# A fused decoder layer on one Trainium2 core: all convolution taps as matmuls, the first B and C and the last expert weights by matmuls, constants over two queues, own places for the end chunks

## What is computed

```
xz = x @ W_in;  x_b, z = split(xz)                      # 256 channels each
xc = silu(conv_b + sum_k xpad[:, k:k+T] * conv_w[:, k])  # 4 taps, causal
proj = xc @ W_xproj                                      # 8 + 16 (B) + 16 (C)
delta = softplus(proj[:8] @ W_dt + b_dt)
h = exp(delta * A) * h + (delta * xc) * B                # per channel and state
y = sum_s h * C + D_param * xc
x = layernorm(x + (y * silu(z)) @ W_out)
...
hidden = silu(x @ gate) * (x @ up)                       # 16 experts of 64
out = sum_e combine[e] * (hidden[e] @ down[e]) + shared expert
```

## Time and profile before

| what | us |
|---|---|
| median of 3 runs (lowest to highest) | 1175.11 (1173.61 to 1177.04) |
| the profiled execution | 1174.27 |
| its span in the trace | 1172.2 |
| PE busy | 1055.3 (90%) |
| DVE busy | 1065.3 (91%) |
| ACT busy | 993.9 (85%) |
| POOL busy | 972.0 (83%) |
| mean granted clock of PE, share of full | 0.967 |

### The profile page before, as it was taken

The page is one execution under the profiler, slowest core; times in us unless marked ns, Lnnn a source line. Parts: engine busy times, 40 slices in busy tenths (PEclk is TensorE's granted clock), DMA queues, the critical chain, the costliest instruction groups (busy, mean ns, idle before and its releaser), DMA issues. The chain is left out here.

```text
span 1172.2 us, 18321 instructions
## 1 busy us (share of the span) xinstructions
PE 1055.3 (90%) x5831; PEld 742.9 (63%) x5831; DVE 1065.3 (91%) x1492; ACT 993.9 (85%) x2176; POOL 972.0 (83%) x590
## 2 busy tenths in 40 slices
PE   4677888989899998989989899998989999898998
PEld 2465665666666666666666666666666667666665
DVE  2999999999999999999999999999999999999622
ACT  6788898989989898998979898898989889898443
POOL 0687888979988897988979798898989889897944
PEclk9677999999999999999989999999999999999999
DMA  6443444545564444555534455654545655443322
GB/s 173 175 171 146 163 164 158 164 164 189 198 196 156 172 162 153 188 207 190 182 127 168 163 189 187 204 175 162 159 160 178 208 187 182 144 166 144 122 68 74
DMA packets 84112, 194.50 MB, mean 166 GB/s; under 512 B 17288, under 2 KB 47936, under 8 KB 67632
## 3 DMA queue, kind: packets, MB, share of 16 engines
q1 hardware_dynamic: 84016, 193.33, 48.8%
HBM read 179.14 MB, written 5.77 MB: 158 GB/s over the span
## 5 line engine op out<-in xcount | busy, mean ns | idle before, releaser
L936 POOL TENSOR_TENSOR read<-state,bc_all 128x1024 f32<-128x1024 f32 x256 | 604.0, 2364 | 140.8 <-DVE state L805 126.3
L805 DVE TENSOR_TENSOR_SCAN state<-decay,drive_bank 128x512 f32<-128x512 f32 (+1 forms) x464 | 594.7, 1313 | 0.4
L755 ACT ACTIVATE decay<-delta,a_neg 128x252 f32<-128x252 f32 x1024 | 424.6, 494 | 0.9
L797 DVE TENSOR_TENSOR drive_bank<-dx_bank,bc_all 128x512 f32<-128x512 f32 (+1 forms) x496 | 328.9, 701 | 27.6 <-DMA bc_all<-bc_dram 25.8
L372 PE MATMUL y_bank<-ident,read 128*128 128x128 f32 x2048 | 282.6, 283 | 44.9 <-POOL read L936 44.8
L372 PEld LDWEIGHTS y_bank<-ident,read 128*128 128x128 f32 x2048 | 241.7, 146 | 118.9 <-POOL read L936 80.8
L977 POOL TENSOR_TENSOR hid<-gu,comb_all 128x512 f32<-128x512 f32 (+1 forms) x136 | 165.0, 1214 | 22.5 <-DVE gu L897 18.8
L363 PEld LDWEIGHTS down_bank<-down_w,hid 128*128 128x128 f32 x1024 | 132.3, 196 | 37.0 <-issue 28.1
L363 PE MATMUL bank<-x2T,gate_w 128*128 128x512 f32 (+1 forms) x272 | 135.0, 588 | 9.8 <-ACT delta L735 4.3
L363 PE MATMUL down_bank<-down_w,hid 128*128 128x128 f32 x1024 | 139.1, 281 | 3.0 <-POOL hid L977 1.4
L363 PE MATMUL bank<-x2T,up_w 128*128 128x512 f32 (+1 forms) x272 | 130.0, 571 | 0.8 <-ACT xc L711 0.7
(11 more groups left out here) (128 smaller groups left out, 1385.0 us busy)
## 6 DMA issues: line engine op xcount, KB each, us to landing
bc_all<-bc_dram SPq DMA_DIRECT2D x128, 1024.0 KB, 5.3
comb_all<-comb_dram SPq DMA_DIRECT2D x240, 128.0 KB, 3.0
x_in<-in_x_dram SPq DMA_DIRECT2D x15, 256.0 KB, 5.7
ctx_in<-in_ctx_dram SPq DMA_DIRECT2D x15, 256.0 KB, 6.4
k_pair<-k_pair SPq DMA_DIRECT2D x30, 128.0 KB, 2.1
q_pair<-q_pair SPq DMA_DIRECT2D x30, 128.0 KB, 2.5
out_dram<-y_out SPq DMA_DIRECT2D x15, 256.0 KB, 3.1
comb_all<-comb_dram SPq DMA_DIRECT2D x32, 64.0 KB, 2.6
```

What stands on the lines that cost most here:

```text
L755: done = e.activation(seqs(decay_t[j % DECAYS][:, i, h, :])[:, :, 1:T], seqs(delta[c % 2][:, h, sub * SUB:(sub + 1) * SUB])[:, :, 1:T], AC ...
L797: e.tensor_tensor(drive_bank[:, a:b, :, :], dx_bank[:, :, :].unsqueeze(1).to_broadcast(shape), bc_all[group % BC_BUFS][:, 0, PAIR * i + a: ...
L805: e.tensor_tensor_scan(states(state_t[j % STATE_BUFS], a, b), states(decay_t[j % DECAYS], a, b), states(drive_bank, a, b), 0.0, ALU.mult, ...
L936: e.tensor_tensor(read_t[j % READS][:, :, :, :], state_t[j % STATE_BUFS][:, :, :, :], bc_all[group % BC_BUFS][:, 1, PAIR * i:PAIR * (i + 1 ...
```

## The change

- **Taps.** w_tap holds both halves; tap_mm is due twice a chunk, four matmuls each. xb_mm, conv_bias, tap1 to tap3 and the conv tile are gone; both xc are one silu with the bias.
- **First B and C.** For the first sub, PE broadcasts the first eight rows (four of B, four of C) of proj to all partitions by matmuls with a column of the identity, into down_bank and y_bank, and DVE copies them to bc_all. proj and the first dx of chunk 0 are made on DVE, dx straight into dx_bank. The first B and C load is gone.
- **Last weights.** In the last chunk the routing weights are spread by matmuls with a selector, built on DVE from the identity, into drive_bank, dx_bank and y_bank; DVE makes the eight hid products there. Its comb store and loads are gone.
- **Constants.** ident, a_log and conv_b are issued by ACT; the rest stays on SP, part of it moved to ticks -15, -7 and 1. The loads have semaphores of their own. Three tiny activations (warm) load function tables early. The centrings move to ticks 7 and 15.
- **Places.** AT has five columns: normal, last, last but one, first, second. EXP_AT too. Four drives of 16 are whole (one before) and four scans (three before).

The diff, cut to its core:

```diff
@@ -42,85 +44,101 @@
-    "tap_mm": [(-38, -40)],
-    "xb_mm": [(-43, -41)],
...
+    "tap_mm": [(-43, -42, -41, -60, -40), (-38, -38, -37, -41, -35)],
+    "xc": [(-36, -35, -39, -29, -44), (-34, -32, -32, -25, -43)],
...
-WHOLE_DRIVES = (7,)
-WHOLE_SCANS = (3, 6, 14)
+WHOLE_DRIVES = (6, 7, 9, 13)
+WHOLE_SCANS = (5, 8, 9, 14)
...
+        selector = decay_t[0][:, :, :, :].rearrange("p i h n -> p (i h n)")
+
+        tap_rows = read_t[0][:, :, :, :].rearrange("p i h n -> p (i h n)")[:, 0:INNER * TAPS]
...
+        def last_weight(pair):
+
+            if pair < PAIR * HALVES:
+                return drive_bank[:, pair // HALVES, pair % HALVES, :]
+            return dx_bank[:, pair % HALVES, :] if pair < PAIR * HALVES + 2 else y_bank[:, pair % HALVES, :]
...
-                for c in due(tick, "tap_mm"):
-                    bank = take(("xb", c, 0), tick, 3)
+                for c, h in due(tick, "tap_mm"):
+                    bank = take(("xb", c, h), tick, 3)
                     w.wait_ge(S["xT"], at(c))
-                    w.wait_ge(S["w_tap"], 1)
+                    w.wait_ge(S["w_tap"], h + 1)
                     for n in range(TAPS):
-                        done = mm(seqs(bank.t[:, 0:width(c)])[:, :, n:T], w_tap[:, TAPS - 1 - n, :],
+                        done = mm(seqs(bank.t[:, 0:width(c)])[:, :, n:T], w_tap[:, h, TAPS - 1 - n, :],
                                   seqs(xT[c % 3][:, 0:width(c)])[:, :, 0:T - n], start=n == 0, stop=n == TAPS - 1)
...
-                for c in due(tick, "xb_mm"):
-                    bank = take(("xb", c, 1), tick, 6)
...
+                    if c == 0:
+                        for two in (0, 1):
+                            for pair in (0, 1):
+                                w.wait_ge(S["bc_copy"], 2 * two + pair - 1)
+                                for i in range(PAIR):
+                                    row = DT_RANK + GROUP * pair + PAIR * two + i
+                                    done = mm((down_bank, y_flat)[pair][:, i * SUB:(i + 1) * SUB],
+                                              ident[0:PROJ, row:row + 1].to_broadcast([PROJ, P]), proj[0:PROJ, 0:SUB])
+                                done.then_inc(S["bc_mm"], 1)
...
+                for c, pair in due(tick, "weight_mm"):
+                    if c < LAST:
+                        continue
+                    w.wait_ge(S["combT"], at(c))
+                    w.wait_ge(S["state"], PAIR * STEPS)
+                    w.wait_ge(S["y_gated"], ALL_SUBS)
+                    w.wait_ge(S["selector"], 1)
+                    mm(last_weight(pair), selector[0:EXPERTS, pair * P:(pair + 1) * P],
+                       combT[:, 0:SUB]).then_inc(S["weight_mm"], 1)
...
+            e.dma_start(ident[:, :], io["c_ident"]).then_inc(S["ident"], 16)
+            e.dma_start(a_log[:, :, :], io["L0_attn_A_log"].rearrange("(h p) n -> p h n", p=P)).then_inc(S["a_log"], 16)
+            per_channel(e, conv_b, io["L0_attn_conv_b"], S["conv_consts"])
...
-            def tap(c, n):
-
-                w.wait_ge(S["conv_bias"], at(c))
...
-                stt(out, seqs(bank_of["xb", c, 1][:, 0:width(c)])[:, :, 0:T - n], conv_w[:, 1, TAPS - 1 - n:TAPS - n], out,
-                    ALU.mult, ALU.add).then_inc(S["conv_tap"], 1)
...
+                    bc_copy(0, 0)
+                    w.wait_ge(S["delta"], 2)
+                    w.wait_ge(S["xc"], HALVES)
+                    e.tensor_tensor(dx_bank[:, :, :], xc[0][:, :, 0:SUB], delta[0][:, :, 0:SUB],
+                                    ALU.mult).then_inc(S["first_dx"], 1)
+                    bc_copy(0, 1)
+                    bc_copy(1, 0)
+                    bc_copy(1, 1)
...
-                        (0, -3, ((w_out[:, :, :], 0, HALVES), (down_w[:, :, :], HALVES, PAIRS))),
-                        (1, 5, ((w_qkv[:, 2:3, :], HALVES + PAIRS, 1), (shared_w[:, 2:3, :], HALVES + PAIRS + 1, 1)))):
+                        (0, 7, ((w_out[:, :, :], 0, HALVES), (down_w[:, :, :], HALVES, PAIRS))),
+                        (1, 15, ((w_qkv[:, 2:3, :], HALVES + PAIRS, 1), (shared_w[:, 2:3, :], HALVES + PAIRS + 1, 1)))):
...
+                    index = pair + 1
+                    w.wait_ge(S["gu"], at(c, index, TILES))
+                    w.wait_ge(S["weight_mm"], pair + 1)
+                    w.wait_ge(S["down_mm"], at(c, index - 3, TILES))
+                    e.tensor_tensor(hid[index % 3][:, 0:SUB], gu[index % 2][:, 0:SUB], last_weight(pair),
+                                    ALU.mult).then_inc(S["last_hid"], 1)
```

More of the change, by code:

```diff
@@ new lines @@
+    "r1_var": [(89, 72, 81, 63, 88)],
+    "ret_copy": [(100, 87, 99, 69, 99)],
+    "square2": [(109, 94, 113, 73, 106)],
+    "normed2": [(115, 100, 115, 87, 111)],
+    "x2T": [(118, 101, 122, 89, 118)],
+    "combT": [(135, 128, 137, 106, 135)],
+    "square3": [(189, 222, 195, 155, 190)],
+    "normed3": [(203, 245, 209, 171, 202)],
+    "delta": [(-20, -20, -16, -18, -11)],
+    "top_tanh": [(130, 117, 126, 101, 130)],
+    "rstd2": [(112, 97, 104, 87, 111)],
+    "rstd3": [(198, 202, 195, 168, 198)],
@@ L288, in blocks_of, with loads @@
             return width(c) // P
+        def loads(buffer, groups):
+            return uses(groups, buffer, BC_BUFS) - (1 if buffer == 0 else 0)
         def uses(before, buffer, buffers):
```

390 lines of the change are left out of this document (208 added, 182 removed), and 5 rows, old and new, of the table EXP_AT.

## The result

The changed kernel takes 1186.6 us (median of 4 runs, 1184.1 to 1195.1), the old one beside it 1174.4 (1168.7 to 1177.0): a ratio of 1.012, 95% interval 1.008 to 1.016. It is slower by 1.2%; forecast was 1145 us. The profiled execution took 1185.05 us, its span is 1183.1. Ratios leave out disturbed executions, of which only e1_one_tap had any: three of its ten, 1803 to 2713 us, the profiled one among them (its median without them is 1177.1).

What follows compares the result with a forecast made beforehand. DVE was taken as the bound: 1172.2 us span, minus 26.1 (middle), minus 4.6 (start), plus 0.4 (tail) gives 1141.9; plus 2.1 and 0.8 to the median, 1144.8, said as 1145 us. Range 1127 to 1161 us.

Steps and rivals of the forecast that it cites:

- DVE's load: Middle: three taps (1.91 us) and merged drives and scans (0.18 us) leave DVE, 66.6 to 64.5 us a chunk.
- With today's 1.9 us of idle the chunk would take 66.4 us: Middle: DVE's lowered load of 64.5 us plus its unchanged idle time gives the new chunk length.
- PE's 66.6 us of busy time would fit: Middle: PE gains 2.5 us a chunk; its matmuls overlap, so only 0.3 us of the gain is given back.
- The bounds: Middle: limits on what PE's added work gives back, 0 to 1.6 us a chunk; 0.3 was taken.
- The comb loads: Middle, SP's queue: moved comb loads change what delays B and C loads; no change taken, bounds half of 25.8 us either way.
- rival (b): Middle: waits for B and C loads shrink by half of 25.8 us and PE's extra work hides; 1128 us, chance 0.13.
- Rival (a): Middle: PE becomes the bound, a chunk takes about 68.0 us; 1164 us, or 1154 with half of that; chance 0.22.
- Rival (d): Middle: two tap groups stall the ring of read buffers, DVE loses 3.4 us a chunk; 1190 us, chance 0.04.
- Start: Before step 8: step 2's drive 6.1 us earlier, second centring costs 1.8, 0.3 won after; 4.6 us won.
- Rival (c): Start gives nothing, through PE's half rate or late constants; 1150 us; chance 0.03 beyond the forecast's range, milder form within it.
- Tail: After the last scan: eight added matmuls (3.4 us on PE) nearly cancel against freed hid products; +0.4 us, bounds -3 and +3.4.
- The signs named: Changed profile: values expected for DVE's conv rows and load, chunk length, PE, POOL's waits, step 2's drive and the last scan.

Runs made afterwards that it cites:

- e1_one_tap: Changed kernel with three of the four tap matmuls of half 1 left out on PE from the third chunk on: 1177.4 us, ratio 0.999 to the old kernel.
- e2: Old kernel without DVE's three convolution multiply-adds from the third chunk on: 1176.1 us, ratio 0.998 to the old kernel.
- e12: Old kernel with expert-weight loads later, logits ahead of y_gated, and without DVE's three convolution multiply-adds from the third chunk on: 1149.6 us, ratio 0.979.
- e3: Old kernel with half 1's x matmul issued four times into the same bank from the third chunk on: 1216.0 us, ratio 1.030.
- e13: Changed kernel with expert-weight loads later, logits ahead of y_gated, and three of half 1's four tap matmuls left out: 1156.4 us, ratio 0.983 to the old kernel.
- e8: Changed kernel with logits ahead of y_gated and the last three expert-weight loads 2, 2 and 8 ticks later: 1167.2 us, ratio 0.993 to the old kernel.
- e9: Old kernel with the last three expert-weight loads of a middle chunk 5, 3 and 4 ticks later: 1153.3 us, ratio 0.981.
- e4: Changed kernel with half 1's convolution back on ACT and DVE from the third chunk on, at its old ticks: 1195.2 us, ratio 1.012 to the old kernel.
- e11: Changed kernel with both centrings of weights on DVE left out: 1179.9 us, ratio 1.004 to the old kernel.
- e7: Changed kernel with the last three expert-weight loads of a middle chunk 2, 2 and 8 ticks later: 1172.9 us, ratio 0.997 to the old kernel.
- e14: Changed kernel with the centrings' separate scaling of row sums removed, the subtraction becoming one scalar_tensor_tensor: 1187.6 us.
- e10: Old kernel with both moves, expert-weight loads later and logits ahead of y_gated: 1151.4 us, ratio 0.979.

## Why the prediction was wrong

**DVE's load: right where it ended, not in what came off.** The sum took 2.1 us a chunk off 66.6; in whole chunks it was 1.3 off 65.8. The three taps were priced at 1.91 us by their starts, and leaving them out took 1.6 us of busy time in e2. ("The same instruction starts 68.5 us later in every repeat" was a misreading as well: nine chunks took 67.2 to 70.0 us, 68.1 in the mean, with DVE idle for 2.4.) ACT lost 3 us a chunk, which gained nothing, as said.

**"With today's 1.9 us of idle the chunk would take 66.4 us": wrong, the step on which the forecast rested.** It took a busy share for a bound. DVE read 66.5 of 68.5, but e2 took 1.6 us of busy time from it and got nothing back. DVE's remaining idle time was not a remainder that stays the same when the work shrinks: most of it (1.8 us a chunk) was the wait for the late loads of B and C, and that wait ends when POOL's hid and SP's queue let it, not when DVE is ready. With the loads on time e12 shows the same: DVE is 65.4 of 65.6 us busy and is not the bound.

**"PE's 66.6 us of busy time would fit": wrong.** The sum gave back 0.3 us of 2.5, because PE read as idle for 4.4 us a chunk. e3 gave 2.2 to 2.6 of 2.5 (part of it perhaps by the delay of half 1's conv), and in the new places 2.1 us of taps cost 1.3 (e13 to e8). About 2.1 to 2.5 us of PE's idle time is no slack, as the runs are read here: PE waits there in order for logits, for copies by ACT, for y_gated. By the code each of these waits starts from a result of PE's own (the router's matmul, the sums, a bank to be copied), so it moves with PE. The other 2.0 us, the wait for POOL's reads, was no room either: in e3 it still stands (17.8 us in nine chunks). It shrinks when the loads are on time (7.5 us in e9). The bounds were set at 0 and 1.6, the upper end from "a third of the 4.4 us that it idles now", which was assumed where the trace had the rows of PE's waits; the logits row alone had 13.7 us in nine chunks.

**The comb loads, "I take no change": right as a difference, wrong as a matter of rank.** The change rid step 12 of its late load, left that of step 14 and shortened the wait from 1.8 to 1.4 us. That this wait was the lock on the chunk was not seen. It stood in the earlier trace rows as the largest wait of DVE, and rival (b) priced the going of half of it at 12.9 us: taking it away gave 22. Rival (b) itself did not happen.

**Rival (a), PE becomes the bound, was the nearest.** It put the chunk at 68.0; it was 68.6: PE's 65.3 (its overlap in the records does count, 66.6 was too high), 2.1 of PE's own waits, not 1.4, and 1.1 for the late load, which (a) left out. That the agreement is one of mechanism is not sure, since e4 takes 68.7 with the old work on PE. Rival (d), the stall of the ring by the two tap groups, is not what happened in the middle: DVE's scans waited for POOL's reads 0.2 us in nine chunks. It shows once, at 221.58, as a wait of 2.47 us. It also gave DVE 12.0 us for three steps, where three sixteenths of a chunk are 12.8. Its total of 1190 us is near the measured one by chance.

The Trainium skill's rule for PE (Perfetto Trace Analysis, Identifying the Most-Contended Engine: judge by the weight loads, not by matmul time) would have said that 65% leaves room. The runs contradict it here: PE's weight loads stood at 64% of the chunk in e3 and 68% in e8 (45.2 us of 70.7, 45.2 of 66.9), and both chunks moved with PE's work.

**Start: -4.6 forecast, +1.7 measured at step 8.** Step 1's scan is 7.4 us earlier than before, at 28.7, where the sum put it at 26.6. Three terms were short. Step 2's drive started at 34.95, not 32.2: 1.5 us were gone by the first drive (23.60 for 22.1), where the last pair of B and C matmuls took 2.07 us at PE's lower clock for 0.9 in the sum; 0.8 came from the scaling's wait for POOL in the first centring, the rest from the scans and drives. The second centring took 3.1 instead of 1.8. And step 8's drive stood idle for 1.63 us, until ACT's copy of the second chunk's dx was done (60.68); the dt matmuls ahead of it ran at the lower clock (3.78 us for two), and the sum had ACT and PE hidden there. Two stretches of the kernel after show the clock, in the B and C matmuls and in the dt matmuls:

```profile
20.00:24.00 4.00, 4.00 (x8) 2.02 (x8) 2.53 (x6) 3.84 (x8) 0.00 (x0) 0.50 0.84 277
54.00:58.00 4.00, 4.00 (x11) 1.93 (x10) 3.96 (x5) 2.17 (x3) 1.17 (x2) 0.50 0.68 238
```

At 0.50 PE runs at 1.2 GHz. Rival (c) named this; it was given too little.

**Steps 8 to 56, another 4.3 us:** not in the forecast, which let the middle begin at once. e11 keeps its lead over the kernel after there. e7 and e8 take 193.6 and 193.9 us from step 8 to step 56, the kernel after 194.9 and the kernel before 190.5; but e14, which changes nothing there, takes 192.8, so a difference of 1 or 2 us between single traces says little. What makes these chunks slow was not isolated: 4.3 of the 10.9 us stay without a shown cause.

**Tail: right in size.** Forecast +0.4, measured +0.5 (71.2 us against 70.7 from the last scan's end). No run tests the two terms that were to cancel.

**The signs named.** Met: no conv row on DVE, DVE's 64.4, the last scan 72.4 us before the end (the last half scan starts at 1110.7). Missed: the chunk (68.6 for 66.5 to 67), PE within 1 us of it (3.5), step 2's drive (34.95 for 30 to 34), POOL's waits for PE (37.4 us for 14 to 30). The last was already the sign of a late PE.

**Open.** Which of the other new places help or harm (e4 says that with the old work they take 0.6 us a chunk more); what holds e10's 65.6 us; and whether it can be shortened on PE's side alone.

## What to carry to other kernels

Before pricing a move of work between two nearly full engines, take the work away from the fuller one without putting it anywhere: if the time stays, as here, the engine is full and not the bound. Look then for the wait that comes once in every period at the same place with the same length; here it was a load standing behind a load that waits for something else, and three numbers in a table were worth 22 us on the old kernel, where the change itself lost 12. Check the stretch, too: cut it where the period starts, and take several. And before calling an engine's idle time room, look at what ends it: in this kernel waits whose end hangs on the engine's own last result moved along with its work.
